# New order tables for the attention of a fused cross-attention and expert feed-forward kernel

## The reference

```
x2 = x + attention(ctx, layernorm(x))       # x: 8 x 512 x 256, ctx: 8 x 1024 x 192
  q = ln(latents) @ Wq.T                    # 4 heads of 64
  k, v = [ln(ctx) @ Wkv.T ; ln(latents) @ Wlkv.T]   # 1024 + 512 = 1536 keys
  qn, kn = rmsnorm(q) * 64**-0.5, rmsnorm(k)
  attn = softmax(where(mask, -max, qn @ kn.T))      # only context keys are masked
  out = attn @ v @ Wo.T + bo
y = x2 + ffn(layernorm(x2))
  logits = rmsnorm(.) @ router.T + bias     # 4096 tokens, 16 experts
  each expert takes its 256 tokens of highest logit (expert choice)
  h = gelu_exact(xe @ fc1.T + b1); out_e = h @ fc2.T + b2
  output[token] = sum(gate * out_e) / sum(gate)
```

## Time and profile before

| | |
|---|---|
| three runs | 1123.39, 1122.91 and 1130.02 us; median 1123.39 |
| profiled execution | span 1127.0 us; of the three runs 1130.02 us fits it, with 3.0 us around the span |
| first scores (scores 0.0.0) | 79.1 us |
| scores 7.0.0, 7.1.0 and 7.1.11 | 744.0, 787.0 and 817.9 us |
| last attention piece of TensorE | 836.9 us |
| first instruction of the search on VectorE | 840.5 us |
| mean granted TensorE clock | 0.957 |
| whole span, busy | TensorE 90%, VectorE 72%, GpSimd 70%, ScalarE 60% |

### The profile page before, as it was taken

One profiled execution on the slowest core, in us unless ns is written; L12 is line 12 of the kernel. 1 busy time (PEld: TensorE's weight loads), 2 busy tenths in 40 slices (PEclk: granted clock), 3 DMA queues, 4 the chain that ended last, 5 costly groups with the idle time before them and its releaser, 6 DMA issues.

```text
span 1127.0 us, 17746 instructions
## 1 busy us (share of the span) xinstructions
PE 1011.0 (90%) x6102; PEld 644.5 (57%) x6102; DVE 808.7 (72%) x1908; ACT 674.0 (60%) x1335; POOL 788.0 (70%) x880
## 2 busy tenths in 40 slices
PE   3789899999999999999999999999851499999996
PEld 3555445555645555564564555444330389999995
DVE  5987667877796796888769577775278776666642
ACT  6666666576576667658566765544436336666662
POOL 3217896787789779689768887988703358777773
PEclk9989999999999999999999999998975599999998
DMA  6020020010012010110110001000118166666662
GB/s 185 7 56 1 6 56 1 24 38 20 1 27 78 1 44 20 39 40 20 44 40 3 1 20 26 2 20 21 32 41 225 63 119 211 214 211 206 198 165 24
DMA packets 73753, 71.94 MB, mean 64 GB/s; under 512 B 38944, under 2 KB 67712, under 8 KB 69568
## 3 DMA queue, kind: packets, MB, share of 16 engines
q1 hardware_dynamic: 66608, 62.05, 17.9%
q0 software_dynamic: 6272, 8.69, 4.5%
q10 hardware_dynamic: 784, 0.07, 0.1%
HBM read 56.96 MB, written 13.83 MB: 63 GB/s over the span
## 4 chain that ended last, share of the span: by engine, by line
PE 76%; DVE 12%; POOL 3%; ACT 3%; DMA 2%; issue 2%; SPq 0%; DVEq 0%; ACTq 0%; POOLq 0%
PE bank L897 40%; PE score_pair L897 18%; PE pair_bank L897 12%; POOL prob_sum L1480 3%; PE bank L930 2%; ACT probs L1207 2%; PE bank L978 2%; DVE c_in L1923 2%; DMA gathered<-rows_scratch,token_index 1%; PE bank L1059 1%; DMA rows_scratch<-all_probs 1%; DVE kc_nat L1777 1%; PE score_pair L1155 1%; DVE qk_nat L1769 1%; DMA x_in<-in_x 1%
## 5 line engine op out<-in xcount | busy, mean ns | idle before, releaser
L1480 POOL TENSOR_TENSOR prob_sum<-prob_sum,probs 128x256 f32<-128x256 f32 x628 | 467.8, 777 | 62.8 <-ACT probs L1207 56.5
L1207 ACT ACTIVATE probs<-score_pair,mask_col 128x512 f32<-128x512 f32 x256 | 161.9, 684 | 112.5 <-PE score_pair L897 109.6
L1802 DVE CUSTOM_DVE_ANT_0 masked_scores<-pair_bank,mask_bias 128x512 bf16<-128x512 f32 x248 | 161.1, 687 | 87.1 <-PE pair_bank L897 86.0
L897 PE MATMUL bank<-probs,v_nat 128*64 128x512 f32 x768 | 204.0, 617 | 0.7 <-ACT probs L1207 0.7
L1207 ACT ACTIVATE probs<-score_pair 128x512 f32<-128x512 f32 x128 | 69.3, 594 | 77.6 <-PE score_pair L897 73.2
L897 PE MATMUL score_pair<-q_hi,k_hi 64*128 64x512 f32 x384 | 92.1, 474 | 14.1 <-ACT probs L1207 12.5
L1795 DVE TENSOR_REDUCE maxima<-pair_bank 128x2 f32<-128x1024 f32 x62 | 75.6, 1219 | 31.5 <-PE pair_bank L897 31.4
L897 PEld LDWEIGHTS score_pair<-q_hi,k_hi 64*128 64x128 f32 x384 | 37.1, 186 | 99.6 <-ACT probs L1207 59.0
L897 PE MATMUL pair_bank<-k_hi,q_hi 64*128 64x512 f32 x372 | 86.9, 462 | 4.4 <-DVE maxima L1802 2.2
L1555 POOL DMA_INDIRECT out_x<-y_out,token_index x32 | 54.7, 1710 | 39.3 <-DVE y_out L2121 34.6
L1458 POOL TENSOR_TENSOR z_lo<-z_full,z_hi 128x512 fp32r<-128x512 f32 x32 | 41.1, 1285 | 55.8 <-ACT z_hi L1207 55.8
(11 more groups left out here) (270 smaller groups left out, 2546.9 us busy)
## 6 DMA issues: line engine op xcount, KB each, us to landing
w_raw<-in_fc SPq DMA_DIRECT2D x16, 1024.0 KB, 4.9
w<-in_fc SPq DMA_DIRECT2D x16, 1024.0 KB, 5.9
c_in<-in_ctx SPq DMA_DIRECT2D x16, 384.0 KB, 3.5
x_in<-in_x SPq DMA_DIRECT2D x8, 512.0 KB, 5.0
out_x<-x_in SPq DMA_DIRECT2D x8, 512.0 KB, 3.0
rows_scratch<-xr_nat SPq DMA_DIRECT2D x8, 512.0 KB, 3.0
c_in<-in_ctx SPq DMA_DIRECT2D x16, 128.0 KB, 3.6
b_rows<-in_fc_bias SPq DMA_DIRECT2D x16, 128.0 KB, 6.0
```

The source lines that it names most:

```text
L897: return pe.matmul(out, lhsT, rhs, start=start, stop=stop, skip_group_check=True)
L1207: return act.activation(out, a, f, bias=bias, scale=scale)
L1480: last = tt(total[:, half], first[:, half], p[:, half], ALU.add)
L1802: last = dve.tensor_tensor_reduce(masked[:, hh, :], place[:, hh, :], mask_bias[:, 512 * g:512 * (g + 1)], 1.0, MASKED, ALU.add, ALU.max, m ...
```

## The change

The diff replaces the numbers of all five tables and writes the period with one more digit. Helpers, buffers, semaphores and the pieces themselves stay as they are, and the same pieces are run. In the code after, the tables take 16 more lines, so that the numbers of all later lines are 16 higher.

```diff
 TENSOR_TIMES = """
-columns:-4059,,,, spread.0.0:-89917,-2148,-2807,-3271,-1523 spread.0.1:-71188,-922,-1500,-1477,287
...
+spread.0.0:138492,43810,-19865,-19852,-19637 spread.0.1:138469,43783,2998,-19709,3130
+spread.1.0:138503,43840,24581,24767,3063 kv.0:138519,43882,24737,24732,24665 spread.1.1:138501,43934,24738,3050,24695
...
 SCALAR_TIMES = """
-w_ctx:-40115,,,, w_lat:-16017,,,, centre_ctx.0:-46322,982,-552,-751,-590 spread.0.0:-33044,3694,267,-242,1723
...
+w_ctx:-10000000007,,,, w_lat:-9999999980,,,, centre_ctx.0:-9999999991,97347,12919,12914,12987
...
-PERIOD = 9515
+PERIOD = 95150
 OWN_TIMES = (0, 1, 2, 2, 2, 2, 3, 4)
```

More of the change, by code:

```diff
@@ new lines @@
+roots.0:206994,112400,155099,112476,112611 roots.1:207008,112411,155115,112485,177539
+roots.2:207031,112430,155122,155131,177554 scale_qk:,177567,155150,155150,177585
+scale_kc.0:207075,177542,155178,155132,177564 scale_kc.1:207123,112434,155186,155168,177625
+prepare_q.0:207199,177591,155190,155196,177627 prepare_k.0.0:207170,177589,155192,155193,177626
+max.0.0.0:207202,177596,155199,155200,177628 max.0.0.1:207202,177601,155246,155214,177633
+prepare_k.0.1:207198,177586,155251,155234,177629 prepare_k.0.2:207207,177598,155253,155204,177717
@@ new lines @@
+first_scale.2:207178,,,, first_scale.1:207181,,,, max.1.1.2:207499,207432,207224,207534,207412
+max.1.2.0:207516,207461,207246,207583,207420 max.1.2.1:207523,207493,207440,207651,207427
+max.1.2.2:207556,207522,207460,207696,207427 max.1.3.0:207572,207583,207495,207761,207464
+max.1.3.1:207588,250201,207590,272696,207465 early_keys:,,,,207611 sum.1.9:,,,,207632
+max.1.3.2:272700,250242,250268,272707,207466 row_max.1:272707,250263,250278,272712,207470
+shift_rows.1:272719,250269,250300,272729,207481 recip.0.0:272761,250362,250357,272785,207484
@@ L287 @@
+route_stats.2:345377,345383,302732,302700,1164945 out.0:302686,302458,302750,302602,1164939
+end_roots.1:,,,302757,1164963 route_stats.0:302712,302624,302759,302640,1164940 end_roots.2:,,,302781,1164963
+scale_logits:368020,367992,368002,1260032,1164963 soft_max:368040,368015,368036,1260088,1164972
+soft:368044,463107,397794,1260117,1164979 sum.1.10:,,,,1164870 sum.1.11:,,,,1164874
 """
 POOL_TIMES = """
[L289 removed]
```

247 lines of the change are left out of this document (123 added, 124 removed).

## The result

The new tables take **1117.35 us** (median of 6 runs, 1114.86 to 1121.48), the old ones 1126.51 (6 runs, 1122.91 to 1130.02). The ratio is 0.991, with a 95% interval of 0.9891 to 0.9928: 9 to 10 us less, half of the 20 us that were forecast and outside the span of 1098 to 1110 of my own case, though inside the full range. The profiled execution has a span of 1115.4 us at a time of 1117.18; so 1.8 us lie around the span. With 1.8 us around its span the old profile was one of 1128.8 us, not the run of 1130.02 that I took it for.

What follows compares the result with a forecast made beforehand. TensorE's own stream was taken to bound 665 of 1127 us. Start and end +1.0 and +1.3, long stage -14.5, batch 7 -8.2 and +0.4 sum to -20.0 from 1123.39: 1103 us, full range 1092 to 1121.

Steps and rivals of the forecast that it cites:

- my own case: Whole kernel: the summed forecast of 1103 us, reaching from 1098 to 1110, chance 0.50.
- The start: Before the first scores: `w_lat` ahead of the first spreads makes low halves late, +1 us (0 to +2.5).
- Part 1: TensorE between 79.1 and 744.0 us: 136 fewer tiling runs at 0.15 to 0.20 us each, -21.7 us.
- The rival of a cheap change: Tilings cost less than read: only 7 of the 21.7 us stay, time 1118 us; chance 0.03.
- Part 2: Between 79.1 and 744.0 us: longer runs delay what other engines wait for, +7.2 us.
- The chain that I had worked out in full: VectorE between units, shift behind `scale_qk`: 17.27 us against TensorE's 16.55, 0.7 us in six batches, +4.2.
- the places to which I gave 0.5 us a batch: Other new waits, such as `max` held by VectorE's reduction or `scores` by ScalarE, followed only in part: +3.0 us.
- Rival (b): Chains eat the tilings' gain: VectorE or GpSimd late by 2.2 to 4 us a batch, about 1115 us; chance 0.23.
- The other signs: TensorE idle below 20 us before scores 7.0.0, wrong above 25; scores 7.0.0 at 729 to 731 us.
- Part 3: Batch 7's first unit: ScalarE's `xr_nat` block and the lower clock go, 43.0 becomes 34.8 us, -8.2.
- Part 4: At the end, `early_keys` saves 1.0, a later reciprocal costs 0.7, batch 6's late row store 1.7: +1.3 with the start.
- rival (c): Slower than before: `shift_rows` behind `scale_qk` puts 2.84 us into the tightest chain, 1137 us; chance 0.09.

Runs made afterwards that it cites:

- run 8: The new tables with `w_lat` moved back behind the first spreads on ScalarE and the first two low halves on GpSimd; 1117.36 us, ratio 0.991 to the old tables.
- Run 2: The kernel of run 1 with 22 stretches of scores, max, values, values split in batches 1 to 6, 44 more tiling changes; 1116.92 us, ratio 0.991.
- run 9: Run 6 and run 7 together without the second maximum's move, plus shift rows ahead of `scale_qk`, `row_max` earlier, last denominators later; 1107.08 us, ratio 0.9819.
- run 4: The new tables with VectorE's scaling of queries and keys cut to 8 of 64 columns of each head from batch 1 on; 1095.57 us, ratio 0.9727.
- run 5: The kernel of run 4 with a VectorE reduction of the other 56 columns before each cut scaling instruction; 1100.27 us, ratio 0.9762.
- run 11: The old tables with VectorE's scaling cut to 8 of 64 columns of each head in batches 1 to 7; 1121.76 us, ratio 0.9946.
- run 7: The new tables with batch 6's probabilities made earlier on VectorE and ScalarE and its rows stored earlier on SyncE; 1112.69 us, ratio 0.9869.
- run 10: The kernel of run 7 with `route_norm` of batch 7 ahead of `soft` of batch 7 on ScalarE; 1113.61 us, ratio 0.9871.
- run 1: The new tables with the first unit's denominators of batches 1 to 6 later in TensorE's order; 1113.49 us, ratio 0.9881.
- run 6: The kernel of run 1 with the keys' low halves and one or two maxima ahead of the reciprocals on VectorE, batches 1 to 6; 1109.97 us, ratio 0.9836.

## Why the prediction was wrong

**The start** (+1, measured -5.5): wrong. I costed the one step that I could see, `w_lat`, which run 8 shows to be worth nothing, and not the order behind it. That the whole came out at even half of the forecast owes 6.5 us to this, and no step of mine foresaw it: it was luck.

**Part 1, the tilings** (-21.7): right. TensorE's busy time fell by 14.4 us in the stage, though more of it ran at half the clock; without that it would be some 19.5 (14.4 and the estimate of 5.1). And summed over all matmuls of the stage, with the mean distance from start to start of each kind behind each kind where nothing waits and the clock is full, the orders should take 650 us and 628. Run 2 put 44 changes back, and each pair cost 0.33 us at its place. The rival of a cheap change is out by these times.

**Part 2, the new waits** (+7.2): this is the step that failed. Time beyond pieces and changes rose by some 19 us, from 14 to 33: 10.7 of that is idle time (12.6 to 23.3), 5.1 the lower clock by the estimate above, and about 3 are not accounted for. The chain that I had worked out in full, the shift behind `scale_qk`, cost 1.6 us and not 4.2, and swapping it back made things worse (run 9). The larger wait came in the places to which I gave 0.5 us a batch without following them: the denominators, reached 1.3 us earlier against the scores (batch 3), met GpSimd's sums, which end 9.0 to 9.4 us behind the start of the unit's last scores (12.8 us in six batches). I had looked at GpSimd's busy share, 82%, and not at when it is done. Rival (b) named it, at about 1115 with 0.23; this is what happened. For the clock I had no term at all: I counted the steady batches at 1.00 and named a fall there only as a sign of being wrong. It fell in four places of the stage, three of them in the steady batches. The other signs stand between: TensorE's idle time is 23.3 us, over the 20 that I expected and under the 25 that I called wrong, and scores 7.0.0 come at 734.8 and not by 731.

Why GpSimd was late is shown by runs 4 and 5: VectorE's scaling stops the sums. The earlier trace rows has 0.72 us a sum (20.03 / 28), and I used it everywhere; four sums a batch take twice that. The old order hid it (run 11: 6 us), the new one brought it onto the path (run 4: 22 us).

**Part 3, batch 7** (-8.2, measured -8.6): the size was right, and the reason half so. ScalarE's block is 4.3 us of it, the larger part of that by the clock, and pieces that moved out of the unit are the rest.

**Part 4, the end** (+1.3, measured +3.7, and +3.3 behind it). The late store of batch 6's rows was the right mechanism and worth 2.5 us (run 7). The longer stretches in search and experts, 3.3 us, I had put at nothing; 2.3 of them, in gates and experts, go with the clock (run 10), and 1.0 up to the first gather, of which run 10 has 0.3 left with the store in time. My own terms for this part add up to +1.4 and not to +1.3, and rival (c)'s 2.84 us should be the 2.91 of the earlier trace rows; neither changes the forecast.

## What to carry to other kernels

When pieces are regrouped on the busiest engine, each piece that moves ahead of another has to be set against the moment at which its producer is done, in us behind a common landmark, and not against the producer's busy share; a piece that in the old order comes just as its input is ready is the first that a regrouping breaks. And after such a piece is put back, the orders of the engines that wait for it have to follow, or the wait only moves (runs 1 and 6). And a wait of some 2 us on the busiest engine can cost more than it lasts: the granted clock of the time behind it belongs to its price.

## What the runs showed of the hardware

Beside VectorE's scaling (128 x 1024 float32, both operands in the tiles' memory) a GpSimd sum takes 1.6 to 1.7 us in place of 0.73. Beside reductions of 128 x 896 from the same tiles it takes 0.745, and beside VectorE's instructions with an operand in a bank 0.73. The scaling itself takes 1.22 us without a sum beside it, and 1.7 with one; a small addition that met a GpSimd product of 1024 columns took 5.11 us. I had not expected that such an interaction decides more than the tilings did.

A change between row tiling and column tiling costs 0.33 us a pair in time that no wait shows.

Behind waits of 1.7 to 2.7 us TensorE's granted clock fell to one half for about 3.4 us in some cases and not in others. Eight matmuls of 256 columns took 3.05 us there and 1.58 at the full clock.
